# Odd chunks of a dense deformable-convolution tap go to the upper 64 columns of TensorE and are merged at the stage's end

## The reference

```
off    = conv3x3(feat, w_off) + b_off             # per pixel and tap: dy, dx (and a mask in block 0)
p[k]   = pixel grid + tap k's place + off[k]      # 9 taps
s[c,k] = bilinear(feat[c], p[k]) (* mask[k])      # 64 channels
out    = einsum('ckhw,ock->ohw', s, w2)           # 64 channels
```

## Time and profile before

| | us |
|---|---|
| two runs | 268.47, 272.05 (median 270.26) |
| span of the profiled execution | 266.8 |
| TensorE matmul busy | 210.1 (79%) |
| VectorE busy | 157.5 (59%) |
| GpSimd busy | 135.4 (51%) |
| ScalarE busy | 117.5 (44%) |

### The profile page before, as it was taken

One profiled execution on the slowest core, in us unless ns is written; L12 is line 12 of the kernel. 1 busy time (PEld: TensorE's weight loads), 2 busy tenths in 40 slices (PEclk: granted clock), 3 DMA queues, 4 the chain that ended last, 5 costly groups with the idle time before them and its releaser, 6 DMA issues. The chain is left out here.

```text
span 266.8 us, 2383 instructions
## 1 busy us (share of the span) xinstructions
PE 210.1 (79%) x794; PEld 109.6 (41%) x794; DVE 157.5 (59%) x270; ACT 117.5 (44%) x159; POOL 135.4 (51%) x127
## 2 busy tenths in 40 slices
PE   8999987698879688196997987869859764999920
PEld 7364963543323233034873655333323231343600
DVE  2966537765857954745266266567486686452271
ACT  2120334877865837001206257648836751023231
POOL 6000017877877878870010077788787787710010
PEclk9999996559999799868999985599979999799955
DMA  7400053332232332230000523223223223310004
GB/s 255 185 0 2 0 158 98 92 95 90 81 98 82 94 92 87 80 98 21 0 0 2 157 75 102 83 79 96 85 82 96 92 80 98 98 42 0 0 0 157
DMA packets 10894, 20.92 MB, mean 78 GB/s; under 512 B 2049, under 2 KB 6402, under 8 KB 10754
## 3 DMA queue, kind: packets, MB, share of 16 engines
q0 software_dynamic: 5376, 14.69, 18.7%
q1 hardware_dynamic: 3282, 4.51, 4.8%
q10 hardware_dynamic: 2224, 1.57, 1.8%
HBM read 17.55 MB, written 3.21 MB: 78 GB/s over the span
## 5 line engine op out<-in xcount | busy, mean ns | idle before, releaser
L326 POOL DMA_INDIRECT G<-table,idx x112 | 128.5, 1148 | 58.3 <-issue 33.5
L562 DVE TENSOR_TENSOR GW<-G,corner_w 128x1024 f32<-128x1024 f32 (+1 forms) x32 | 34.9, 1091 | 51.8 <-DMA G<-table,idx 50.9
L951 PE MATMUL ps<-first,GS 128*128 128x128 f32 x64 | 15.7, 332 | 37.5 <-DVE GS L577 37.5
L761 ACT ACTIVATE sT<-ps 128x256 f32<-128x256 f32 x32 | 12.2, 380 | 64.9 <-PE ps L951 64.9
L906 PE MATMUL ps<-x,V 128*64 128x512 f32 x64 | 36.8, 705 | 0.0
L731 ACT ACTIVATE near_y<-ps,dbias 128x1024 f32<-128x1024 f32 x32 | 35.4, 1105 | 1.5 <-PE ps L898 1.5
L313 POOL TENSOR_TENSOR rstd<-var,half_neg 64x1 f32<-64x1 f32 (+1 forms) x4 | 2.6, 639 | 63.1 <-DVE var L376 41.0
L734 ACT ACTIVATE hat_y<-near_y 128x1024 f32<-128x1024 f32 x32 | 33.8, 1057 | 1.0
L807 PE MATMUL ps<-first 128*128 128x128 f32 x180 | 28.7, 317 | 0.0
L807 PEld LDWEIGHTS ps<-first 128*128 128x128 f32 x180 | 25.9, 225 | 4.2 <-issue 3.9
L951 PEld LDWEIGHTS ps<-first,GS 128*128 128x128 f32 x64 | 7.0, 154 | 45.5 <-DVE GS L577 44.5
(11 more groups left out here) (132 smaller groups left out, 234.4 us busy)
## 6 DMA issues: line engine op xcount, KB each, us to landing
G<-table,idx POOLq DMA_INDIRECT x112, 2.9
second<-in_second SPq DMA_DIRECT2D x1, 1552.5 KB, 8.5
table<-feat_t ACTq DMA_DIRECT2D x2, 512.0 KB, 4.8
table<-feat_t SPq DMA_DIRECT2D x2, 512.0 KB, 4.8
out<-x SPq DMA_DIRECT2D x4, 256.0 KB, 2.2
x<-in_x ACTq DMA_DIRECT2D x1, 512.0 KB, 4.4
x<-in_x SPq DMA_DIRECT2D x1, 512.0 KB, 5.2
first<-in_first SPq DMA_DIRECT2D x1, 224.0 KB, 4.0
```

The source lines that it names most:

```text
L326: pool.indirect_dma_start(out=G[:, done % RING, k, :], out_offset=None, in_=table[b], in_offset=bass.IndirectOffsetOnAxis(ap=idx[b][:, n:n ...
L562: dve.tensor_tensor(GW[:, :, k0:k1].rearrange("p c k e -> p k c e"), G[:, (b * TILES + t) % RING, k0:k1].rearrange("p k (c e) -> p k c e", ...
L761: act.activation(sT[:, t % 2, 2 * part:2 * part + 2], ps[:, B_ST[part], 0:2 * P] .rearrange("p (q n) -> p q n", n=P), ACT.Copy).then_inc(s ...
L951: mm = pe.transpose(ps[:, B_ST[part], q % 2 * P:(q % 2 + 1) * P], GS[:, t % 2, k:k + 2, :].rearrange("p k e -> p (k e)"), ident)
```

## The change

Chunks with an odd number write to `ps[64:128, ...]`, the same two banks, through columns 64 to 127 of the array. Chunks 0 and 1 both start an accumulation. A new tile `upper` and a semaphore `s_upper` are added. At unit MERGE = 14, behind its transposes, TensorE waits for ScalarE's copy of the upper partitions and adds it to the lower ones with two matmuls by the identity. `s_c2`'s first count now comes with the first of these, no longer with the last chunk.

```diff
+MERGE = 14
...
+        upper = sb("upper", [P, N])
...
+        s_upper = sem("s_upper")
...
                 for u in range(UNITS):
                     for c in chunks_at(u + AHEAD):
                         chunk(b, c)
+                    if u == MERGE:
+                        act.wait_ge(s_dense, (b + 1) * CHUNKS)
+                        act.activation(upper[HID:P], ps[HID:P, B_C1:B_C1 + 2, :].rearrange("p h n -> p (h n)"),
+                                       ACT.Copy).then_inc(s_upper, 1)
                     if u == UNITS - 1 and b:
                         hidden(0)
...
                 def dense(c):
                     pe.wait_ge(s_S, b * CHUNKS + c + 1)
+                    side = slice(c % 2 * HID, (c % 2 + 1) * HID)
                     for h in range(2):
-                        mm = pe.matmul(ps[0:HID, B_C1 + h, :], V[:, c % TILES, c // TILES, :],
-                                       half(S[(b * CHUNKS + c) % SRING], h), start=(c == 0),
-                                       stop=(c == CHUNKS - 1 and h == 0))
-                        if c == CHUNKS - 1 and h == 0:
+                        mm = pe.matmul(ps[side, B_C1 + h, :], V[:, c % TILES, c // TILES, :],
+                                       half(S[(b * CHUNKS + c) % SRING], h), start=(c < 2),
+                                       stop=(c == CHUNKS - 1))
+                    mm.then_inc(s_dense, 1)
+
+                def merge():
+                    pe.wait_ge(s_upper, b + 1)
+                    for h in range(2):
+                        mm = pe.matmul(ps[0:HID, B_C1 + h, :], ident[HID:P, HID:P],
+                                       half(upper[HID:P], h), start=False, stop=(h == 0))
+                        if h == 0:
                             mm.then_inc(s_c2[b + 1], 1)
-                    mm.then_inc(s_dense, 1)
...
                     mm.then_inc(s_st, 1)
+                    if u == MERGE:
+                        merge()
                     if u < BESIDE.index(1):
                         keep_clock(0, IDLE[8 + u])
                     positions(u)
```

## The result

The change made the kernel slower. The first comparison gave a median of 274.09 us against 270.26, a ratio of 1.022 (95% interval 1.016 to 1.028). A second one, with six runs against 21 of the kernel before, gave 276.10 against 268.56 us: 1.030 (1.026 to 1.035). The forecast was 271.5 us. Medians are of all executions of a kernel, ratios of those within 1.5% of its fastest, so the two don't match exactly.

What follows compares the result with a forecast made beforehand. GpSimd's gathers were taken to pace each deform stage, so only the tails counted: block 1 +1.5 us and block 0 -0.3 gave +1.2, added to the 270.26 us median for 271.5 us. The range was 268.4 to 274.7 us.

Steps and rivals of the forecast that it cites:

- The bound: Both gather stages: GpSimd's gathers set the pace, so TensorE time saved in mid-stage is worth 0 on the path.
- between none and one record: Dense chunks: overlap between column halves hides at most one record, up to 0.87 us at half clock, 0.45 at full.
- rival 2: Column halves run fully side by side, 2x; block 0 gives 0.5 us back, block 1 nothing: +0.7, 271.0 us; chance 0.12.
- -0.3: Block 0's tail: the merge fills the hole, the clock holds, and the statistics' matmul comes 0.3 us earlier.
- +1.2 us: Whole kernel: the forecast sum, +1.5 for block 1's tail and -0.3 for block 0's.
- Rival 3: Both tails begin at half clock because chunks are less busy, 2.5 us more in each: 276.5 us; chance 0.07.
- Its counter: Block 0's tail: argument against the half-clock start, that TensorE has no pause from 113.2 on even with one record less.
- the stated range: Whole kernel: time after the change expected from 268.4 to 274.7 us.
- rival 1: Clock falls in block 0's tail as before, or another stretch gets half clock: +3.0, 273.3 us; chance 0.20.
- The merge's own time: Both tails: four identity-matmul records taken as 1.91 us, from the last conv3; bounds 0 and 3.8 us.
- Block 0's late statistics: Block 0's tail: statistics wait for the merge, so unit 15's weighting is 1.5 us late, 1.0 with one record saved.
- +1.5 forecast: Block 1's tail: merge of 1.91 us less 0.43 slack delays the last transposes and the kernel's end; bounds 0 and +3.4.

Runs made afterwards that it cites:

- experiment 1: The changed kernel without copy and merge (odd chunks missing from the output), against the kernel before: 269.16 against 269.13 us, ratio 1.001.
- Experiment 10: The change plus eight filler matmuls in each block where TensorE waits for GS of unit 14, against the kernel before: 271.26 against 268.87 us, 1.008.
- Experiment 9: The change with both chunks of a pair on the same column side, merges kept, against the kernel before: 272.63 against 268.87 us, 1.014.
- experiments 10 and 11: The change with fillers ahead of both merges, then also with block 0's first-half statistics behind unit 15's GS, against the kernel before: 271.26 and 269.42 us.
- experiment 8: The kernel before plus eight filler matmuls behind block 0's transposes of unit 14, against the kernel before: 269.95 us, 1.006.

## Why the prediction was wrong

- **The bound: right.** GpSimd's gathers pace both stages, with the same 33.5 us between them, and TensorE's saved time in mid-stage is worth nothing (experiment 1).
- **The overlap: wrong, and this is where it starts.** The prediction took "between none and one record". It was the whole chunk: eight records in 3.46 us, which is 3.5 us saved where a whole pair runs at the half clock. (In block 0's tail it could be only some 2 us, and rival 2's 3.5 was too much, since the clock of the earlier trace rows rises under chunk 15.) The prediction had this as its second rival and priced it 0.5 us *faster*, since it asked only what the shorter work does to the order of the waits. The Trainium skill's "TensorEngine Tiling (Array Packing)", Key Properties, has different tiles executing in parallel: the traces agree. By the Trainium skill's "TensorE: Matmul & The Clock Gate", Part 3, matmuls keep their order; here chunk 15's first record, behind four of chunk 14's in the program, starts 0.01 us after chunk 14's first. The measurement decides.
- **"I take -0.3, since the hole is the only thing ahead of the fall": the failed term.** The merge was to fill a hole and hold the clock. But the overlap opens a new hole ahead of the merge, where none was counted, and in block 1 the sum had no term for the clock at all: +1.2 us was forecast, and the medians are 3.8 and 7.5 us apart. The clock fell behind the hole in three of the four tails of the change's two traces, under the merge or its contracts (2.3, 3.6 and 3.6 us for the merge); the fourth, block 1 in the first trace, kept the full clock. Rival 3, given 0.07 and 276.5 us, comes nearest, but it had the clock still low when the tails begin. In both traces it was back at full ahead of block 0's transposes of unit 14 (1.00 from 120 to 122 us in the first, from 118 to 120 in the second) and fell later; that 276.5 lies near the second median of 276.1 is in part luck. Its counter, "even one record less still leaves TensorE without a pause from 113.2 on", holds up to the end of the dense work but not for the stretch behind it. Experiment 10 shows that the clock is the cause: keep both parts and fill the hole, and the loss falls from 2.2 or 3.0% to 0.8%. Experiment 9 supports the overlap's part in it: take the overlap away, keep the merge, and 1.4% is left, clear of the second comparison but not of the first.
- **Where the number was near, it was luck.** Block 0 of the first trace ends 0.1 us late, against a forecast of 0.3 us early, but the clock did not hold through 124 to 128 us as forecast (0.60 from 124 to 126); it fell earlier and came back earlier. The first median, 274.1 us, lies just inside the stated range, whose upper end was worked out for another case (rival 1 with a high draw).
- **The merge's own time: right.** 1.86 us in place of the 1.91 taken from the last conv3, at the full clock. The ScalarE copy took 1.02 us where 1.1 was taken.
- **Block 0's late statistics: mechanism right.** In the profile after, they start at 121.98 and the weighting at 122.70, 1.0 us late, the figure given for one record saved. With the clock held, putting them late is worth about 1.2 us (experiments 10 and 11). The -0.3 set against it assumed the clock's fall of one profiled execution to be the rule; experiment 8 found no gain in filling that hole.
- **Block 1: +1.5 forecast.** The last transposes are 2.3 us late in the profile after: 0.5 from a later GS, and 1.8 rather than 1.5 from the merge. The 0.43 us taken off as slack was the idle time of the weight loads; the matmuls of the earlier trace rows were idle for only 0.19 us before 238.26. The block alone costs 0.8%, 2.2 us. Where the clock fell, in the second trace, the stretch from the transposes of unit 14 to those of unit 15 grew by 5.1 us.
- **The kernel's last matmuls** ran 1.15 us longer in the profile after, since the clock fell while they ran. The prediction had no step for it. That the change causes it isn't shown: over the profiles of all kernels these matmuls took 3.69 to 5.82 us, the longest in the kernel before with fillers.

Open: why the change in both blocks costs more than the sum of its parts, by half in the first comparison and by double in the second. The clock is the likely link, since the first block's delay shifts when the second block's tail meets it, but no run separates that. The size differs too between the two comparisons of the change, 1.022 and 1.030, with intervals that just overlap. And idle time ahead of a merge doesn't settle alone whether the clock falls: 1.03 us was enough in one profile and 2.23 us was not in another.

## What to carry to other kernels

Work that leaves a busy engine off the critical path isn't free to leave: ask what the engine will do in the time it saves, and whether the clock that it was granted is still there when the next critical piece arrives. A piece that is added (here a merge) belongs where its engine waits for something else already, one or two units ahead of the tail. When two parts of a change are each nearly harmless, test them together: here overlap alone cost nothing measurable (0.1%), merge alone 1.2%, and both 2 to 3%.

## What the runs showed of the hardware

- fp32 matmuls that use columns 0 to 63 and 64 to 127 of the array run side by side, also when they stand several records apart in the program. A pair of chunks takes 3.46 us at the half clock, as one chunk does (3.47), and 1.77 us at the full clock (231.60 to 233.37 in the second comparison's profile). A chunk in the upper columns also overlaps the contracts in the lower ones behind it, here at 59.7 us of the kernel after:

```profile
59.70 0.64 PE L914 MATMUL ps<-x,V 128*64 128x512 f32 x1
59.71 0.65 PE L934 MATMUL ps<-sT,second 128*64 128x128 f32 x4
60.17 1.45 PE L914 MATMUL ps<-x,V 128*64 128x512 f32 x3
```

- With less time busy, TensorE was granted less. The mean clock of a whole execution was 0.82 to 0.84 in all eight executions of the change, and 0.86 to 0.89 in the 21 of the kernel before beside them. Over the two gather stages of one profile each it went from 0.83 and 0.88 to 0.77 and 0.79 (after):

```profile
38.00:120.00 82.00, 58.98 (x201) 26.48 (x200) 55.79 (x76) 49.18 (x64) 64.17 (x56) 0.77 0.30 89
153.00:235.00 82.00, 59.83 (x201) 27.26 (x200) 52.77 (x74) 46.71 (x59) 64.35 (x56) 0.79 0.30 89
```

- Once it had fallen at the transposes ahead of a merge, the clock stayed low for a while although TensorE was busy throughout: in the second comparison's profile it is 0.50 in every window from 122 to 134 us, in which TensorE was idle for 0.5 us.
